# All pair products of 40 projected features: features projected in place, three store slots of 87 pairs, loads as whole 20 KB rows

## The chip, the cores and the metric

The kernel runs on one core of one Trainium2 chip. The metric is the device time in microseconds (us); of the kernel before there are three runs, with a median of 511.1 us.

## The reference

`r_x` holds 512 examples of 40 features with 128 numbers each, in fp32, and `L0_rec_W` is a 128x128 matrix. Each feature is projected by the matrix, and then each of the 780 pairs of features of an example is multiplied element by element.

```
proj = jnp.einsum('bnd,ed->bne', x, W)          # x: (512, 40, 128), W: (128, 128)
out  = proj[:, PAIR_I, :] * proj[:, PAIR_J, :]  # PAIR_I, PAIR_J = np.triu_indices(40, k=1)
```

The output has 512 x 780 x 128 numbers, 204.47 MB; the input has 10.49 MB.

## The kernel before

The 512 examples are four tiles of 128, with an example on each partition. A tile's 40 features are taken from the last to the first, in 20 groups of two. For each group TensorE transposes the two features against an identity (L172), ScalarE carries the result out of PSUM into `x_turned` (L206), TensorE multiplies it by the transposed matrix `w_turned` (L182), and ScalarE carries the projected features into `proj` (L217). VectorE then forms the pairs (L248): one instruction multiplies feature i by a run of features j, in as many pairs as fit.

The 780 pairs of a tile go out as 20 chunks of 39 pairs, also from the last to the first. A chunk is formed in one of five buffers, the slots `products0` to `products4` (19,968 bytes a partition), and SyncE issues its store when VectorE has finished it (L143 waits for `chunk_ready`, L145 issues). VectorE waits at the start of a chunk until the store that last used the slot has landed (L265, L271). So a store is 128 rows of 19,968 bytes, and there are 80 of them.

The input is loaded into `x_in`, which has two halves, one for even tiles and one for odd, in pieces of four features: 128 rows of 2,048 bytes, ten pieces a tile. SyncE issues the 20 pieces of the first two tiles at the start (L137). The pieces of the third and fourth tile are issued by ScalarE between its copies, each as soon as the groups of the piece before in that half have been turned (L211). `proj` has two halves as well. VectorE gives a half of it back when it has formed the tile's last chunk (L257), and ScalarE waits for that before it starts on the tile that will use the half (L205).

The matrix `w_in` is loaded by the first DMA of ScalarE (L199); TensorE transposes it (L162), ScalarE copies it (L201), and TensorE starts on the first group only when that copy is done (L163).

Two hardware DMA queues are in use, SyncE's (q1 in the profile) and ScalarE's (q10). A DMA of 128 rows is spread over 16 DMA engines, so that each engine has eight rows of it.

Of the kernel before, what the change touches and what calls it, by code (L numbers as in the profile page):

```python
# [5 lines left out]
P = 128  # L25
FEATURES = 40
DIM = 128
# [3 lines left out]
LOAD_FEATURES = 4  # L31
LOADS = FEATURES // LOAD_FEATURES
# [3 lines left out]
GROUPS_PER_LOAD = LOAD_FEATURES // GROUP  # L36

CHUNK = 39
CHUNKS = PAIRS // CHUNK
SLOTS = 5  # L40
ROUNDS = CHUNKS // SLOTS

assert LOADS * LOAD_FEATURES == FEATURES and GROUPS * GROUP == FEATURES
assert CHUNKS * CHUNK == PAIRS and ROUNDS * SLOTS == CHUNKS and GROUPS % 2 == 0
assert GROUP <= BANK_FEATURES and LOAD_FEATURES % GROUP == 0


def load_range(load):

    return FEATURES - (load + 1) * LOAD_FEATURES, FEATURES - load * LOAD_FEATURES  # L50


def group_range(group):

    return FEATURES - (group + 1) * GROUP, FEATURES - group * GROUP


def chunk_range(chunk):

    return PAIRS - (chunk + 1) * CHUNK, PAIRS - chunk * CHUNK  # L60


def chunk_rows(chunk):

    low, high = chunk_range(chunk)
# [8 lines left out]
def group_of(i):  # L74

    return (FEATURES - 1 - i) // GROUP


def groups_for(chunk):

    return group_of(chunk_rows(chunk)[-1][0]) + 1 if chunk >= 0 else 0


def pairwise_products(nc, x, w, out):
# [3 lines left out]
    assert x.shape[0] == tiles * P and tiles % 2 == 0 and tiles >= 4  # L88

    with ExitStack() as ctx:  # L90
# [17 lines left out]

# [6 lines left out]

        x_loaded = [[sem(f"x_loaded{half}_{k}") for k in range(LOADS)] for half in range(2)]
# [9 lines left out]
        proj_free = sem("proj_free")  # L126
# [32 lines left out]
        def _(pe):  # L159
            pe.wait_ge(identity_made, 1)  # L160
            pe.wait_ge(w_loaded, 16)
            pe.transpose(w_ps[:, :], w_in[:, :], identity[:, :]).then_inc(w_in_ps, 1)  # L162
            pe.wait_ge(w_ready, 1)  # L163

            def turn(pair, half, group):

                if group % GROUPS_PER_LOAD == 0:

                    pe.wait_ge(x_loaded[half][group // GROUPS_PER_LOAD], 16 * pair + 16)
                a, b = group_range(group)  # L170
                for n in range(a, b):
                    last = pe.transpose(turned_ps[group % 2][:, n - a, :], x_in[half][:, n, :], identity[:, :])  # L172
                last.then_inc(group_turned, 1)
# [121 lines left out]
```

## Time and profile before

| | |
|---|---|
| device time, median of 3 runs | 511.1 us (510.85 to 511.14) |
| profiled execution, first to last instruction (its span) | 508.2 us |
| difference between the two | 2.9 us |
| VectorE busy | 437.3 us (86% of the span) |
| TensorE busy | 71.3 us (14%) |
| ScalarE busy | 54.3 us (11%) |
| moved by DMA | 215.10 MB, 423 GB/s over the span |

The profile gives only the span of the profiled execution, so its time is taken as the span and the 2.9 us that the median run has beyond it. "Busy" counts the time in which an engine executes. The line of DMA digits gives the mean busy share of the 16 DMA engines in 40 slices of 12.7 us; "GB/s" is what they moved in each slice. A share can be a few hundredths above 1, since successive packets of one DMA engine overlap a little.

### The profile page before, as it was taken

To read this page: it belongs to the slowest core of one execution; us is meant where nothing else is said; L and a number is where in the kernel's file an instruction comes from. 1 tells how busy PE (TensorE), PEld (TensorE's weight loads), DVE (VectorE), ACT (ScalarE), POOL (GpSimd) and SP (SyncE) were. 2 spreads that over 40 slices of the span, in tenths; PEclk is the share of its full clock that TensorE was granted. 3 is DMA by queue.
4 is the path that set the end of the run, shared out by engine and by line. 5 is a ranking of instruction groups with operands and counts; after the bars stand their busy time and mean duration, and the time that the engine had idled before them with its cause. 6 is when DMAs were issued, how large, how long until landed. Compare 5 with 4: busy or idle time off the path is not lost.

```text
span 508.2 us, 2204 instructions
## 1 busy us (share of the span) xinstructions
PE 71.3 (14%) x481; PEld 65.4 (13%) x481; DVE 437.3 (86%) x220; ACT 54.3 (11%) x162; POOL 0.7 (0%) x6
## 2 busy tenths in 40 slices
PE   6965100000930000000660000000000000000000
PEld 5854100000920000000660000000000000000000
DVE  3999988888999999899999999999899989999900
ACT  5752000000720000000450000000000000000000
POOL 0000000000000000000000000000000000000000
PEclk9995555555875555555695555555555555555555
DMA  8999999999999999999999999999999999999996
GB/s 311 411 423 433 427 431 428 430 431 434 428 431 432 434 431 432 431 429 434 434 430 432 431 434 432 431 432 432 429 434 431 427 427 427 429 429 431 431 431 277
DMA packets 17430, 215.10 MB, mean 423 GB/s; under 512 B 1936, under 2 KB 2064, under 8 KB 7184
## 3 DMA queue, kind: packets, MB, share of 16 engines
q1 hardware_dynamic: 14400, 209.72, 96.7%
q10 hardware_dynamic: 3024, 5.31, 2.8%
q8 instruction: 2, 0.03, 0.0%
q14 instruction: 4, 0.03, 0.0%
HBM read 10.55 MB, written 204.47 MB: 423 GB/s over the span
## 4 chain that ended last, share of the span: by engine, by line
DMA 68%; DVE 21%; issue 5%; PE 1%; DVEq 0%; SPq 0%; ACT 0%; ACTq 0%
DMA out_dram<-products 67%; DVE products L248 21%; DMA w_in<-in_L_rec_W_dram 1%; PE proj_ps L182 0%; PE turned_ps L172 0%; SPq L145 0%; DVEq L248 0%; PE w_ps L162 0%; ACT proj L217 0%; ACT x_turned L206 0%; DVEq L271 0%; ACT w_turned L201 0%; SPq L144 0%; DVEq L247 0%; ACTq L205 0%
## 5 line engine op out<-in xcount | busy, mean ns | idle before, releaser
L248 DVE TENSOR_TENSOR products<-proj 128x384 f32 (+36 forms) x220 | 437.3, 2045 | 46.3 <-DMA out_dram<-products 37.3
L182 PE MATMUL proj_ps<-w_turned,x_turned 128*128 128x128 f32 x320 | 60.5, 319 | 181.5 <-ACT x_turned L206 181.3
L182 PEld LDWEIGHTS proj_ps<-w_turned,x_turned 128*128 128x128 f32 x320 | 48.9, 219 | 186.3 <-ACT x_turned L206 184.4
L206 ACT COPY x_turned<-turned_ps 128x256 f32<-128x256 f32 x80 | 30.0, 379 | 174.0 <-DVEq L257 171.9
L172 PE MATMUL turned_ps<-identity,x_in 128*128 128x128 f32 x160 | 34.4, 306 | 5.7 <-ACT proj L217 5.1
L217 ACT COPY proj<-proj_ps 128x256 f32<-128x256 f32 x80 | 29.7, 373 | 31.4 <-issue 19.0
L172 PEld LDWEIGHTS turned_ps<-identity,x_in 128*128 128x128 f32 x160 | 23.1, 161 | 6.6 <-issue 5.3
L201 ACT ACT_TABLE_LOAD x1 | 1.3, 1283 | 1.2 <-PEq L284 1.2
L162 PE MATMUL w_ps<-identity,w_in 128*128 128x128 f32 x1 | 0.4, 447 | 4.1 <-DMA w_in<-in_L_rec_W_dram 4.1
L162 PEld LDWEIGHTS w_ps<-identity,w_in 128*128 128x128 f32 x1 | 0.2, 182 | 4.0 <-issue 4.0
L201 ACT COPY w_turned<-w_ps 128x128 f32<-128x128 f32 x1 | 0.3, 265 | 2.1 <-PE w_ps L162 2.1
L155 POOL TENSOR_SCALAR_AFFINE_SELECT identity<-identity 128x128 f32<-128x128 f32 x1 | 0.3, 292 | 0.2 <-POOL identity L153 0.2
L153 POOL MEMSET identity<- 128x128 f32 x1 | 0.2, 204 | 0.3 <-POOLq L284 0.3
L284 POOL MEMSET const-bfloat16-1.0<- 128x1 bf16 x1 | 0.1, 101 | 0.0
L284 POOL MEMSET const-uint8-127<- 128x1 uint8 x1 | 0.1, 101 | 0.0
L284 POOL MEMSET const-float32-0.0<- 128x1 f32 x1 | 0.1, 98 | 0.2 <-issue 0.2
L284 POOL MEMSET const-float32-1.0<- 128x1 f32 x1 | 0.1, 98 | 0.0
## 6 DMA issues: line engine op xcount, KB each, us to landing
out_dram<-products SPq DMA_DIRECT2D x80, 2496.0 KB, 24.0
x_in<-in_r_x_dram SPq DMA_DIRECT2D x20, 256.0 KB, 6.1
x_in<-in_r_x_dram ACTq DMA_DIRECT2D x20, 256.0 KB, 29.8
w_in<-in_L_rec_W_dram ACTq DMA_DIRECT2D x1, 64.0 KB, 3.2
```

Source lines behind the costliest of these rows:

```text
L153: pool.memset(identity[:, :], 0.0).then_inc(identity_zeroed, 1)
L155: pool.affine_select(out=identity[:, :], in_=identity[:, :], compare_op=ALU.not_equal, fill=1.0, base=0, pattern=[[-1, P]], channel_multip ...
L162: pe.transpose(w_ps[:, :], w_in[:, :], identity[:, :]).then_inc(w_in_ps, 1)
L172: last = pe.transpose(turned_ps[group % 2][:, n - a, :], x_in[half][:, n, :], identity[:, :])
L182: last = pe.matmul(proj_ps[group % 2][:, k, :], x_turned[group % 2][:, k, :], w_turned[:, :], start=True, stop=True)
L201: act.copy(w_turned[:, :], w_ps[:, :]).then_inc(w_ready, 1)
L206: act.copy(x_turned[group % 2][:, :, :], turned_ps[group % 2][:, 0:GROUP, :]).then_inc(x_turned_ready, 1)
L217: act.copy(proj[:, half, a:b, :], proj_ps[group % 2][:, 0:GROUP, :]).then_inc(proj_ready, 1)
L248: last = dve.tensor_tensor(products[slot][:, place:place + count, :], proj[:, tile % 2, i:i + 1, :].broadcast_to([P, count, DIM]), proj[:, ...
L284: nc = _bacc.Bacc("TRN2", target_bir_lowering=False, num_devices=1)
```

## The change

The kernel after has one tile `feats` with two halves in place of `x_in` and `proj`: a tile is loaded into a half, and ScalarE writes each projected group over the loaded features of that group, which TensorE has already transposed. The pairs are formed from there. The freed memory goes to the slots: three of 87 pairs (44,544 bytes a partition) in place of five of 39.

Tiles 1 to 3 go out as nine chunks each, six of 87 pairs and three of 86. Tile 0 goes out as 15 chunks that grow from 30 to 69 pairs. That is 42 stores. The loads are 6: features 36 to 39, 28 to 35 and 0 to 27 of tile 0 (rows of 2,048, 4,096 and 14,336 bytes), and tiles 1, 2 and 3 whole (rows of 20,480 bytes). SyncE issues all of them. Those of tiles 2 and 3 come right behind the last store of tile 0 and of tile 1, since the half is free only when VectorE has formed all pairs of the tile in it. ScalarE issues only the matrix. `proj_free` is gone, and with it ScalarE's wait for it.

TensorE now transposes the first group before it waits for the matrix copy (`w_ready`). Its loop and those of SyncE and ScalarE over the tiles are written out; VectorE keeps a loop over tiles 1 to 3.

Of TensorE, ScalarE and VectorE the diff below shows only what is added; the lines that go are in the listing above.

```diff
-LOAD_FEATURES = 4
-LOADS = FEATURES // LOAD_FEATURES
...
-CHUNK = 39
-CHUNKS = PAIRS // CHUNK
-SLOTS = 5
-ROUNDS = CHUNKS // SLOTS
...
+FIRST_LOADS = [(36, 40), (28, 36), (0, 28)]
+SLOTS = 3
+FIRST_SIZES = [30, 34, 38, 41, 44, 47, 50, 53, 56, 59, 62, 64, 66, 67, 69]
+SIZES = [87] * 6 + [86] * 3
+SLOT_PAIRS = max(FIRST_SIZES + SIZES)
+FIRST_ROUNDS = len(FIRST_SIZES) // SLOTS
+ROUNDS = len(SIZES) // SLOTS
...
-        x_in = [sbuf(f"x_in{h}", [P, FEATURES, DIM]) for h in range(2)]
-        proj = sbuf("proj", [P, 2, FEATURES, DIM])
-        products = [sbuf(f"products{s}", [P, CHUNK, DIM]) for s in range(SLOTS)]
+        feats = sbuf("feats", [P, 2, FEATURES, DIM])
+        products = [sbuf(f"products{s}", [P, SLOT_PAIRS, DIM]) for s in range(SLOTS)]
...
-        x_loaded = [[sem(f"x_loaded{half}_{k}") for k in range(LOADS)] for half in range(2)]
+        first_loaded = [sem(f"first_loaded{k}") for k in range(len(FIRST_LOADS))]
+        tile_loaded = [sem(f"tile_loaded{half}") for half in range(2)]
...
-        proj_free = sem("proj_free")
...
-            for half in range(2):
-                for load in range(LOADS):
-                    a, b = load_range(load)
-                    sp.dma_start(x_in[half][:, a:b, :],
-                                 x[half * P:(half + 1) * P, a:b, :]).then_inc(x_loaded[half][load], 16)
-            with sp.Fori(0, tiles) as tile:
-                for chunk in range(CHUNKS):
-                    a, b = chunk_range(chunk)
-                    sp.wait_ge(chunk_ready, tile * CHUNKS + (chunk + 1))
-                    sp.nop(nofuse=True)
-                    sp.dma_start(out[bass.ds(tile * P, P), a:b, :],
-                                 products[chunk % SLOTS][:, :, :]).then_inc(stored[chunk % SLOTS], 16)
+            for k, (a, b) in enumerate(FIRST_LOADS):
+                sp.dma_start(feats[:, 0, a:b, :], x[0:P, a:b, :]).then_inc(first_loaded[k], 16)
+            sp.dma_start(feats[:, 1, :, :], x[P:2 * P, :, :]).then_inc(tile_loaded[1], 16)
+            done = 0
+            for tile in range(tiles):
+                for k, (a, b) in enumerate(first_chunks if tile == 0 else chunks):
+                    done += 1
+                    sp.wait_ge(chunk_ready, done)
+                    sp.dma_start(out[tile * P:(tile + 1) * P, a:b, :],
+                                 products[k % SLOTS][:, 0:b - a, :]).then_inc(stored[k % SLOTS], 16)
+                if tile + 2 < tiles:
+                    sp.dma_start(feats[:, tile % 2, :, :],
+                                 x[(tile + 2) * P:(tile + 3) * P, :, :]).then_inc(tile_loaded[tile % 2], 16)
             for slot in range(SLOTS):
-                sp.wait_ge(stored[slot], 16 * tiles * ROUNDS)
+                sp.wait_ge(stored[slot], 16 * (FIRST_ROUNDS + (tiles - 1) * ROUNDS))
...
+            def turn(half, group):
...
                 a, b = group_range(group)
                 for n in range(a, b):
+                    last = pe.transpose(turned_ps[group % 2][:, n - a, :], feats[:, half, n, :], identity[:, :])
                 last.then_inc(group_turned, 1)
+            def project(before, group):
...
+            def last_banks_left(before):
+                pe.wait_ge(proj_ready, before + GROUPS)
+            pe.wait_ge(identity_made, 1)
+            pe.wait_ge(w_loaded, 16)
+            pe.transpose(w_ps[:, :], w_in[:, :], identity[:, :]).then_inc(w_in_ps, 1)
+            starts = {group_of(b - 1): k for k, (a, b) in enumerate(FIRST_LOADS)}
+            pe.wait_ge(first_loaded[0], 16)
+            turn(0, 0)
+            pe.wait_ge(w_ready, 1)
+            for group in range(1, GROUPS):
+                if group in starts:
+                    pe.wait_ge(first_loaded[starts[group]], 16)
+                turn(0, group)
+                project(0, group - 1)
+            project(0, GROUPS - 1)
+            last_banks_left(0)
+            for tile in range(1, tiles):
+                pe.wait_ge(tile_loaded[tile % 2], 16 * ((tile + 1) // 2) if tile % 2 else 16 * (tile // 2))
+                turn(tile % 2, 0)
+                for group in range(1, GROUPS):
+                    turn(tile % 2, group)
+                    project(tile * GROUPS, group - 1)
+                project(tile * GROUPS, GROUPS - 1)
+                last_banks_left(tile * GROUPS)
...
...
+                act.wait_ge(group_projected, tile * GROUPS + group + 1)
+                act.copy(feats[:, tile % 2, a:b, :], proj_ps[group % 2][:, 0:GROUP, :]).then_inc(proj_ready, 1)
+            for tile in range(tiles):
+                carry_turned(tile, 0)
                 for group in range(1, GROUPS):
+                    carry_turned(tile, group)
+                    carry_projected(tile, group - 1)
+                carry_projected(tile, GROUPS - 1)
...
...
+            def multiply_chunk(tile, k, low, high, seen):
+                for i, j, count, place in chunk_rows(low, high):
+                    if group_of(i) >= seen:
+                        seen = group_of(i) + 1
+                        dve.wait_ge(proj_ready, tile * GROUPS + seen)
                     last = dve.tensor_tensor(
+                        products[k % SLOTS][:, place:place + count, :],
+                        feats[:, tile % 2, i:i + 1, :].broadcast_to([P, count, DIM]),
+                        feats[:, tile % 2, j:j + count, :], ALU.mult)
                 last.then_inc(chunk_ready, 1)
+                return seen
+            seen = 0
+            for k, (low, high) in enumerate(first_chunks):
+                if k >= SLOTS:
+                    dve.wait_ge(stored[k % SLOTS], 16 * (k // SLOTS))
+                seen = multiply_chunk(0, k, low, high, seen)
             with dve.Fori(1, tiles) as tile:
+                seen = 0
+                for k, (low, high) in enumerate(chunks):
+                    dve.wait_ge(stored[k % SLOTS],
+                                16 * ROUNDS * tile + 16 * (FIRST_ROUNDS - ROUNDS + k // SLOTS))
+                    seen = multiply_chunk(tile, k, low, high, seen)
```

SyncE's queue at the start, before. `x_in` are the loads, `products` the chunks of pairs on their way to the output, and 128x512 means 512 numbers on each partition:

```order
L131 UNCONDITIONAL_BRANCH [waits barrier_Pool_Activation_PE_DVE_SP_release]
L137 DMA x_in<-in_r_x_dram 128x512 x20
L140 UNCONDITIONAL_BRANCH
L140 ISA
L145 ISA [waits chunk_ready]
L145 DMA out_dram<-products 128x4992
L143 REGISTER_ALU
```

SyncE's queue at the start, after, up to the third store:

```order
L107 UNCONDITIONAL_BRANCH [waits barrier_Pool_Activation_PE_DVE_SP_release]
L110 DMA feats<-in_r_x_dram 128x512
L110 DMA feats<-in_r_x_dram 128x1024
L110 DMA feats<-in_r_x_dram 128x3584
L111 DMA feats<-in_r_x_dram 128x5120
L118 DMA out_dram<-products0 128x3840 [waits chunk_ready]
L118 DMA out_dram<-products1 128x4352 [waits chunk_ready]
L118 DMA out_dram<-products2 128x4864 [waits chunk_ready]
```

Twenty equal loads have become four, with the same bytes, and the first store is of 3,840 numbers a partition in place of 4,992.

SyncE's queue after, from the end of tile 0 to the load of tile 3:

```order
L118 DMA out_dram<-products 128x8576
L118 DMA out_dram<-products 128x8832
L122 DMA feats<-in_r_x_dram 128x5120
L118 DMA out_dram<-products 128x11136 x6
L118 DMA out_dram<-products 128x11008 x3
L122 DMA feats<-in_r_x_dram 128x5120
```

The loads of tiles 2 and 3 stand between stores on the same queue, where before they were on ScalarE's queue.

ScalarE's queue at the start, before (`turned_ps` and `proj_ps` are the PSUM tiles of the transposes and of the projection):

```order
L199 DMA w_in<-in_L_rec_W_dram 128x128
L201 ACT_TABLE_LOAD
L201 COPY w_turned<-w_ps 128x128 [waits w_in_ps]
L230 UNCONDITIONAL_BRANCH
L206 COPY x_turned<-turned_ps 128x256 [waits group_turned,proj_free]
L206 COPY x_turned<-turned_ps 128x256 [waits group_turned]
L211 DMA x_in<-in_r_x_dram 128x512
L217 COPY proj<-proj_ps 128x256 [waits group_projected]
```

ScalarE's queue at the start, after:

```order
L183 DMA w_in<-in_L_rec_W_dram 128x128
L185 ACT_TABLE_LOAD
L185 COPY w_turned<-w_ps 128x128 [waits w_in_ps]
L189 COPY x_turned<-turned_ps 128x256 [waits group_turned] x2
L195 COPY feats<-proj_ps 128x256 [waits group_projected]
```

The load between the copies is gone, and so is the wait for `proj_free`; the copies themselves stand as before.

## Rows read from the trace of the kernel before

**Rows 1.** The page: busy share by engine and by slice.
```profile
PE 71.3 (14%) x481; PEld 65.4 (13%) x481; DVE 437.3 (86%) x220; ACT 54.3 (11%) x162; POOL 0.7 (0%) x6
DMA  8999999999999999999999999999999999999996
GB/s 311 411 423 433 427 431 428 430 431 434 428 431 432 434 431 432 431 429 434 434 430 432 431 434 432 431 432 432 429 434 431 427 427 427 429 429 431 431 431 277
```

**Rows 2.** Waits of VectorE: who waited for whom, total us, times, longest us.
```profile
DVE products L248 <- DMA out_dram<-products: 37.3, 64, 1.4
DVE products L248 <- ACT proj L217: 8.9, 2, 7.9
```

**Rows 3.** Windows: us, busy time by engine, granted PE clock, DMA share, GB/s.
```profile
0.00:1.70 1.70, 0.00 (x0) 0.00 (x0) 0.00 (x0) 0.52 (x1) 0.70 (x6) 1.00 0.00 0
1.70:3.00 1.30, 0.00 (x0) 0.00 (x0) 0.00 (x0) 0.77 (x1) 0.00 (x0) 1.00 0.75 203
3.00:6.00 3.00, 1.41 (x5) 0.90 (x5) 0.00 (x0) 0.45 (x2) 0.00 (x0) 1.00 0.99 343
6.00:18.00 12.00, 11.90 (x90) 11.37 (x90) 9.11 (x12) 9.59 (x30) 0.00 (x0) 1.00 1.05 393
18.00:30.00 12.00, 11.20 (x91) 10.10 (x90) 12.00 (x8) 9.53 (x30) 0.00 (x0) 1.00 1.04 423
60.00:110.00 50.00, 0.00 (x0) 0.00 (x0) 43.06 (x19) 0.00 (x0) 0.00 (x0) 0.50 1.01 429
118.00:240.00 122.00, 17.46 (x120) 16.41 (x120) 111.47 (x57) 13.43 (x40) 0.00 (x0) 0.56 1.01 432
...
390.00:495.00 105.00, 0.00 (x0) 0.00 (x0) 86.19 (x35) 0.00 (x0) 0.00 (x0) 0.50 1.01 429
503.00:504.00 1.00, 0.00 (x0) 0.00 (x0) 0.00 (x0) 0.00 (x0) 0.00 (x0) 0.50 0.38 160
...
506.00:507.00 1.00, 0.00 (x0) 0.00 (x0) 0.00 (x0) 0.00 (x0) 0.00 (x0) 0.50 0.05 20
```

**Rows 4.** The page: DMA queues with packets, MB and share of 16 engines.
```profile
q1 hardware_dynamic: 14400, 209.72, 96.7%
q10 hardware_dynamic: 3024, 5.31, 2.8%
```

**Rows 5.** Loads: instructions on ScalarE's queue (ns, first to last start), and issue to landing.
```profile
L211 ACTq DMA_DIRECT2D x_in<-in_r_x_dram x20: 334/335/5746, 6.2 to 49.4; - x20
...
DMA to landing us min/median/max: 3.0/7.9/65.5
```

**Rows 6.** VectorE's largest and smallest common instruction by form: busy us, mean ns, idle.
```profile
L248 DVE TENSOR_TENSOR products<-proj 128x4992 f32 x3 | 16.1, 5358 | 1.8 <-DMA out_dram<-products 1.8
...
L248 DVE TENSOR_TENSOR products<-proj 128x384 f32 x24 | 13.3, 554 | 4.7 <-DMA out_dram<-products 4.7
```

**Rows 7.** Timeline of the opening: start us, us, engine, instruction, idle before.
```profile
0.74 0.41 ACTq L199 DMA_DIRECT2D w_in<-in_L_rec_W_dram  x1
0.75 9.87 SPq L137 DMA_DIRECT2D x_in<-in_r_x_dram  x20
...
5.04 1.11 PE L172 MATMUL turned_ps<-identity,x_in 128*128 128x128 f32 x4 [0.53 <-ACT w_turned L201]
...
9.18 54.29 DVE L248 TENSOR_TENSOR products<-proj 128x256 f32<-128x256 f32 x34 [0.99 <-ACT proj L217]
...
10.74 0.38 PE L172 MATMUL turned_ps<-identity,x_in 128*128 128x128 f32 x2
...
15.13 43.55 SPq L145 DMA_DIRECT2D out_dram<-products  x9
```

**Rows 8.** Timeline of VectorE alone, 0 to 30 us.
```profile
9.18 21.59 DVE L248 TENSOR_TENSOR products<-proj 128x256 f32<-128x256 f32 x18 [0.99 <-ACT proj L217]
```

**Rows 9.** The longest wait of ScalarE: total us, times, longest us.
```profile
ACT x_turned L206 <- DVEq L257: 171.9, 2, 101.9
```

More of the change, by code:

```diff
@@ L35, with group_of, chunk_ranges, chunk_rows @@
 GROUPS = FEATURES // GROUP
-GROUPS_PER_LOAD = LOAD_FEATURES // GROUP
-CHUNK = 39
-CHUNKS = PAIRS // CHUNK
-SLOTS = 5
-ROUNDS = CHUNKS // SLOTS
[L43 to L50, printed above, removed]
+FIRST_LOADS = [(36, 40), (28, 36), (0, 28)]
[5 more added lines that the diff above has]
+ROUNDS = len(SIZES) // SLOTS
+assert sum(FIRST_SIZES) == PAIRS and sum(SIZES) == PAIRS
+assert FIRST_ROUNDS * SLOTS == len(FIRST_SIZES) and ROUNDS * SLOTS == len(SIZES)
+assert GROUPS * GROUP == FEATURES and GROUPS % 2 == 0 and GROUP <= BANK_FEATURES
 def group_range(group):
     return FEATURES - (group + 1) * GROUP, FEATURES - group * GROUP
[L58 to L65, printed above, removed]
+def group_of(i):
+    return (FEATURES - 1 - i) // GROUP
+def chunk_ranges(sizes):
+    ranges, high = [], PAIRS
+    for size in sizes:
+        ranges.append((high - size, high))
+        high -= size
+    return ranges
+def chunk_rows(low, high):
     rows = []
@@ L71, in chunk_rows @@
     return rows
[L74 to L81, printed above, removed]
 def pairwise_products(nc, x, w, out):
@@ L159, in _ @@
         def _(pe):
[L160 to L169, printed above, removed]
+            def turn(half, group):
                 a, b = group_range(group)
                 for n in range(a, b):
-                    last = pe.transpose(turned_ps[group % 2][:, n - a, :], x_in[half][:, n, :], identity[:, :])
+                    last = pe.transpose(turned_ps[group % 2][:, n - a, :], feats[:, half, n, :], identity[:, :])
                 last.then_inc(group_turned, 1)
-            def project(pair, half, group):
-                before = pair * 2 * GROUPS + half * GROUPS
+            def project(before, group):
                 pe.wait_ge(x_turned_ready, before + (group + 1))
@@ L184, in project @@
                 last.then_inc(group_projected, 1)
-            with pe.Fori(0, tiles // 2) as pair:
-                for half in range(2):
-                    turn(pair, half, 0)
-                    for group in range(1, GROUPS):
-                        turn(pair, half, group)
-                        project(pair, half, group - 1)
-                    project(pair, half, GROUPS - 1)
-                    pe.wait_ge(proj_ready, pair * 2 * GROUPS + (half + 1) * GROUPS)
+            def last_banks_left(before):
[22 more added lines that the diff above has]
+                last_banks_left(tile * GROUPS)
         @block.scalar
@@ L201, in _, with carry_turned @@
             act.copy(w_turned[:, :], w_ps[:, :]).then_inc(w_ready, 1)
-            def carry_turned(pair, half, group):
-                act.wait_ge(group_turned, pair * 2 * GROUPS + (half * GROUPS + group + 1))
+            def carry_turned(tile, group):
+                act.wait_ge(group_turned, tile * GROUPS + group + 1)
                 act.copy(x_turned[group % 2][:, :, :], turned_ps[group % 2][:, 0:GROUP, :]).then_inc(x_turned_ready, 1)
-            def load_ahead(pair, half, load):
-                a, b = load_range(load)
-                act.dma_start(x_in[half][:, a:b, :],
-                              x[bass.ds(pair * 2 * P + (half + 2) * P, P), a:b, :]).then_inc(x_loaded[half][load], 16)
@@ L230, in _, with carry_projected @@
-            with act.Fori(0, tiles // 2 - 1) as pair:
-                for half in range(2):
-                    carry_tile(pair, half, loads=True)
-            for half in range(2):
-                carry_tile(tiles // 2 - 1, half, loads=False)
+            def carry_projected(tile, group):
+                a, b = group_range(group)
+                act.wait_ge(group_projected, tile * GROUPS + group + 1)
+                act.copy(feats[:, tile % 2, a:b, :], proj_ps[group % 2][:, 0:GROUP, :]).then_inc(proj_ready, 1)
@@ L237, in _ @@
+            for tile in range(tiles):
+                carry_turned(tile, 0)
+                for group in range(1, GROUPS):
+                    carry_turned(tile, group)
+                    carry_projected(tile, group - 1)
+                carry_projected(tile, GROUPS - 1)
         @block.vector
         def _(dve):
-            def multiply_chunk(tile, chunk):
-                slot = chunk % SLOTS
-                first_group = groups_for(chunk - 1)
-                for i, j, count, place in chunk_rows(chunk):
-                    group = group_of(i)
-                    if group >= first_group:
-                        first_group = group + 1
-                        dve.wait_ge(proj_ready, tile * GROUPS + (group + 1))
+            def multiply_chunk(tile, k, low, high, seen):
[3 more added lines that the diff above has]
+                        dve.wait_ge(proj_ready, tile * GROUPS + seen)
```

29 lines of the change are left out of this document (2 added, 27 removed).

## The prediction

> **What bounds the kernel now.** I began with the page's busy shares and slices. VectorE is busy 86%, but the DMA digits stand at 9 in all slices but the first and last, at 427 to 434 GB/s from the fourth on [rows 1]. The waits of VectorE say who leads: it waited 64 times for stores to free a slot, 37.3 us in all, and for projected features only at the very start [rows 2]. VectorE is ahead and the DMA engines are never let go, so the time is bytes over rate, plus the time before the first byte and an uneven end. The windows tell the rate of each stretch [rows 3]: nothing moves before 1.7 us; 2,048-byte load rows alone go at 393 GB/s; stores with such rows among them at 429; stores alone at 432; and in the last quarter at 429 without loads. After 503 us the share falls to 0.38, and at 506 to 507 it is 0.05, less than one of 16 engines (0.06): the engines stop on average near 504, and one works on past 507.
>
> The queue table gives the rows [rows 4]. q1's 14,400 packets are 80 stores x 128, 20 loads x 128 and 100 x 16 completions, so a row of 19,968 bytes is one packet today. The byte count barely changes, so the change can only win by fewer rows, by smoother stretches, or at the ends.
>
> **The change part by part.** Sums are made in the profiled span, 508.2 us; the median of 511.1 is 2.9 above it, which I keep.
>
> Price of a row. Per engine (a sixteenth of the rate), 19,968 bytes at 432 GB/s take 739.6 ns and 2,048 bytes at 393 take 83.4 ns. From 60 to 110 us one load goes with each store: the last of ScalarE's loads, issued at 49.4, landed 65.5 us later [rows 5], which is the time of ten such pairs. Eight rows of each at 429 GB/s take 6.569 us; less 8 x 739.6, 0.653 is left, 81.6 ns a short row. The line through 81.6 and 739.6 is 0.03672 ns a byte and 6.4 ns fixed a row; through 83.4 the fixed part is 8.4. It is zero if the store rate is a ceiling that longer rows don't lift. I take 6.4, nearest to the row that has stores in it.
>
> Stores: 10,240 rows become 42 x 128 = 5,376. That is 4,864 fewer, 304 an engine: -1.9 us (0 to -2.6). A row of 44,544 bytes should take 1,642 ns, 434 GB/s.
>
> First loads (tiles 0 and 1): 160 rows an engine at 83.4 ns are 13.3 us; after, 327,680 bytes in 32 rows, 12.0 + 0.2 = 12.2: -1.1 (0 if 393 GB/s belongs to reading and not to short rows).
>
> Later loads (tiles 2 and 3): 160 x 81.6 = 13.1 us become 16 rows, 12.0 + 0.1: -0.9 (+0.3 if reads go at 393, 13.3 us).
>
> Smoother stretches: 18 to 30 us ran at 423 where stores with loads give 429, which costs 0.2; with one data queue I count it gone (0 to -0.2). 390 to 495 ran at 429 in place of 432, 0.7 us; nothing in these rows explains it, so I take half, -0.4 (0 to -0.7).
>
> By a rule of the Trainium skill (DMA: Bandwidth & Descriptors, "Why small descriptors are slow (HBM only)") a packet has about 3 cycles of overhead on top of its 32-byte beats. As an estimate from that page's 850 MHz, 3.5 ns a row, and a 2,048-byte row would take 67 cycles, 79 ns; the trace has 81.6 and 83.4, so it bears out the kind and not the size. By the rule all row savings together come to 2.0 us and the time to about 508.5; the sum goes by the rows.
>
> The opening. The bytes still come first. By 6.0 us the windows of before have moved 0.26 + 1.03 = 1.29 MB [rows 3]; the other 4.02 of 5.31 MB (tiles 0, 1 and the matrix) take 9.3 us at 434, so loads end at 15.3. VectorE: 128x4992 takes 5,358 ns and 128x384 554 [rows 6], 1.0425 ns an element or 0.1334 us a pair. Eighteen merged instructions with 19,456 elements take 21.59 us [rows 8]; less 20.28, that is 0.07 for each. I leave the second product at 9.18 [rows 7]. It could come 0.5 earlier, since group 0's transposes need no longer wait for the matrix copy (0.53 at 5.04 [rows 7]); it could come 0.6 later, since the matrix's eight rows an engine now pass among 4,096-byte rows. The first 30 pairs then end at 9.18 + 29 x 0.1334 + 7 x 0.07 + 0.1 = 13.6. Issue adds 0.2, and 1.0 passes from issue to first byte (0.75 to about 1.7 [rows 3, 7]): 14.8, before 15.3. From there a pair costs DMA 0.151 us and VectorE 0.133 plus three or four instructions a chunk:
>
> | chunk | pairs | fit to move at | DMA free at |
> |---|---|---|---|
> | 1 | 34 | 19.7 | 19.8 |
> | 2 | 38 | 25.0 | 25.0 |
> | 3 | 41 | 30.8 | 30.8 |
> | 4 | 44 | 36.9 | 37.0 |
>
> After that the lead grows. It is tight to a tenth, so I put +0.1; one microsecond of delay at 9.18 would cost about one here, so +2 is the other end. The later loads cannot be late for TensorE: group 6, the first of the 28-feature load, was turned at 10.74 [rows 7], and that load ends at 6.0 + 1.4 MB / 434 = 9.2; even two microseconds there are hidden, since VectorE wants those features only in chunk 2.
>
> Three slots. A slot's round is three stores of 13.2 us, 39.5. In it stand the store, VectorE's 87 x 0.1334 plus up to 14 instructions, 12.6, and 1.5 of notice and issue: 27.3. The 12 us left also cover the spread of about 4 between first and last engine. Cost nothing; if this cover went, each us would show once a round.
>
> In place. Tile 2 can load only after tile 0's last pairs, near 115 us (its stores end near 133). Behind those stores it lands near 140, and turning it takes about 30. ScalarE was idle 101.9 us at a stretch for the half that VectorE held [rows 9]; VectorE needs tile 2 near 245. Slack 75 us, cost nothing. The two loads stand ahead of no store that is ready, being issued right behind one. The written-out loops of TensorE and ScalarE lie under that slack; `nop` and register work on SyncE lie in its waits for VectorE.
>
> Sum: -1.9 -1.1 -0.9 -0.2 -0.4 +0.1 = -4.4; span 503.8. The 2.9 on top gives 506.7; I round by the likelier small gain at the end to 506.6.
>
> **The rivals.**
> Reads are slow in themselves. For it: 393 GB/s is the only stretch of loads alone. Against: with stores they cost 81.6 ns a row, so most of it is the row. Then -1.9 +0 +0.3 -0.2 -0.4 = -2.2 (no idle gap, since loads end later): 508.9.
>
> The last engine comes nearer the others. It trails the mean by over 3 us, and the early stretch where two queues shared engines is one source. If half goes: 505.0.
>
> Rows of 44 KB are not moved whole. For: nothing longer than 19,968 bytes is seen. Against: those go whole. Cut in two or three, stores gain nothing: 508.5.
>
> The matrix is late. The landing of 65.5 us shows the queues taking turns row by row: 8 rows of a load needed a whole store each. Should the matrix's eight rows meet 20,480-byte rows (753 ns) and not short ones, it comes 8 x 0.67 = 5.4 us late, less 0.5 of slack: +4.9 -4.4, so 511.6. Against: its issue at 0.74 is ahead of SyncE's third [rows 7]. The Trainium skill (same page, "Queues, rings and completion order") has an engine drain a whole packet, typically 9 to 17 descriptors, from one ring before it turns to the next; by that the matrix would pass in one turn and this rival is nearly empty. The trace's alternation disagrees, so I keep it.
>
> The slower side: long store rows hold a lower rate. Place: every store; the seed of it is the 429 of the last quarter [rows 3]. Stores take 474.7 us today at their mean of 430.7 GB/s. All else gains 2.1, so it decides below 204.47 / 476.8 = 428.8 GB/s; at 426 they take 480.0, +5.3 -2.1: 514.3.
>
> **How the numbers follow.** Forecast 0.60 (own range 505.4 to 508.2), slow reads 0.12, nearer last engine 0.12, cut rows 0.05, late matrix 0.05, lower rate 0.06. The range 504.0 to 509.8 leaves out the last two and a little at the low edge. A change under 0.2%, 1.0 us, can't be told from none here. Faster by more: the first four less a little, 0.85; within: the late matrix and edges, 0.08; slower 0.07.
>
> **What would show it.** The load stretch from 6 to 14 us at about 430 GB/s rather than 393 (slow reads if not); stores at 434; q1 packets 42 x 128 + 6 x 128 + 48 x 16 = 6,912 (cut rows if more); the second product at 9.18 within 0.6 (late matrix if not); first store data at 15; no DMA share under 0.9 from 15 to 45 us; VectorE still waiting for stores; the last engine about 3 us behind. The forecast is wrong if VectorE waits for features after the opening or the store rate stays at 432 or below.

## The result and the profile after

| | before | after |
|---|---|---|
| device time, median | 511.06 us | 506.73 us (506.18 to 507.04, 4 runs) |
| ratio to before, 95% interval | | 0.9915 (0.9902 to 0.9927) |
| span of the profiled execution | 508.2 us | 504.4 us |

The change makes the kernel 4.3 us (0.85%) faster; 506.6 was forecast. The forecast of the span was 503.8.

Not all of the gain lies in the span. The runs of the kernel before that were timed beside the edits below have a median span of 508.6 to 508.7, with 2.2 us around it. The four runs of after have a median span of 504.9, with 1.8 us around it. So the span is 3.8 us shorter, and 0.4 us is saved outside it, as in every edit below. The 2.9 us that the forecast kept came from 508.2 and 511.1, a span and a median of different executions; the profiled execution of before had the shortest span of all that are listed.

The page of the kernel after, as in [rows 1], and its DMA queues, as in [rows 4]:

```profile
PE 66.4 (13%) x481; PEld 60.9 (12%) x481; DVE 431.6 (86%) x191; ACT 54.7 (11%) x162; POOL 0.7 (0%) x6
DMA  8999999999999999999999999999999999999997
GB/s 350 428 435 425 429 434 432 444 428 437 384 404 439 442 424 435 442 435 419 440 421 455 413 439 445 420 435 441 433 423 440 442 424 435 442 427 429 440 443 307
...
q1 hardware_dynamic: 6912, 214.96, 99.3%
q10 hardware_dynamic: 144, 0.07, 0.0%
```

The packet count is the 6,912 that the forecast gave for rows moved whole: 42 stores and 6 loads of 128 rows, and 48 x 16 completions. So 44,544-byte rows go as one packet. The GB/s of single slices scatter more than before, since a packet is now up to 1.6 us long and counts whole where it starts (0.7 us before). The same holds at the edges of every stretch below, so a rate over 30 us can be off by 2 to 3%. Two slices, the eleventh and twelfth (126 to 151 us), are lower than scatter explains: 384 and 404.

The stretches of after (length, busy time by engine, granted clock, DMA share, GB/s), to be laid beside [rows 3]:

```profile
1.70:3.00 1.30, 0.00 (x0) 0.00 (x0) 0.00 (x0) 0.74 (x1) 0.00 (x0) 1.00 0.77 222
3.00:6.00 3.00, 1.87 (x7) 1.33 (x8) 0.00 (x0) 0.98 (x3) 0.00 (x0) 1.00 1.07 412
6.00:14.00 8.00, 8.00 (x59) 7.73 (x58) 5.60 (x9) 5.87 (x19) 0.00 (x0) 1.00 1.01 434
14.00:30.00 16.00, 15.29 (x124) 13.82 (x122) 16.00 (x13) 13.24 (x42) 0.00 (x0) 1.00 1.02 432
60.00:110.00 50.00, 0.00 (x0) 0.00 (x0) 50.00 (x18) 0.00 (x0) 0.00 (x0) 0.50 1.01 433
118.00:150.00 32.00, 6.33 (x33) 5.92 (x34) 32.00 (x20) 3.53 (x10) 0.00 (x0) 0.52 1.02 414
150.00:240.00 90.00, 11.00 (x90) 10.16 (x88) 78.16 (x30) 9.91 (x31) 0.00 (x0) 0.59 1.00 433
270.00:360.00 90.00, 14.64 (x114) 13.75 (x112) 74.59 (x23) 12.58 (x38) 0.00 (x0) 0.59 1.00 434
390.00:495.00 105.00, 0.00 (x0) 0.00 (x0) 79.19 (x25) 0.00 (x0) 0.00 (x0) 0.50 1.00 434
474.40:504.40 30.00, 0.00 (x0) 0.00 (x0) 2.33 (x1) 0.00 (x0) 0.00 (x0) 0.50 0.89 386
```

and two stretches of the kernel before that [rows 3] has not:

```profile
118.00:150.00 32.00, 17.46 (x120) 16.41 (x120) 29.30 (x22) 13.43 (x40) 0.00 (x0) 0.71 1.00 431
...
478.20:508.20 30.00, 0.00 (x0) 0.00 (x0) 5.36 (x1) 0.00 (x0) 0.00 (x0) 0.50 0.86 367
```

The loads of the opening go at 434 GB/s in place of 393. Stores alone go at 433 to 434 in place of 432, and the 429 of the last quarter is gone. From 118 to 150 us the rate is 414, where before it was 431: by these rates 32 x (431 - 414) / 431 = 1.3 us are lost there. In it lie the last store of tile 0 and the load of tile 2 behind it. And the end is shorter: in the last 30 us before it moved 367 x 30 = 11.0 MB and after 11.6, which at 434 GB/s is 1.3 us less idling.

The edges can be taken out: the trace has a start, a duration and a size for each packet, so its bytes can be spread evenly over its duration. The time lost in a stretch is then its length less its bytes at 434 GB/s. In us ("the rest to 470" is 150 to 235 and 290 to 470 us):

| lost against 434 GB/s | 0 to 14 | 14 to 115 | 115 to 150 | 235 to 290 | the rest to 470 | from 470 | sum |
|---|---|---|---|---|---|---|---|
| before | 3.8 | 1.9 | 0.25 | 0.3 | 1.9 | 4.4 | 12.6 |
| after | 2.8 | 0.9 | 2.05 | 0.2 | 0.3 | 2.6 | 8.8 |

The difference of the sums, 3.8 us, is that of the two spans. So the stretch with the load of tile 2 costs 1.8 us more than before, and the end 1.9 less. The loss with the load is sharply placed. The store rows of 35,328 bytes that start between 132 and 133 us take 1.94 us in the mean where 1.31 is usual. The load's rows of 20,480 bytes take 0.78 us between 136 and 138, but 1.1 to 1.2 between 138 and 140; those of the next load that start from 259 to 265 us take 0.76 to 0.78.

VectorE in the opening and its waits, as in [rows 7, 8] and [rows 2]:

```profile
7.13 0.29 DVE L212 TENSOR_TENSOR products<-feats 128x128 f32<-128x128 f32 x1 [7.13 <-ACT feats L195]
8.41 0.89 DVE L212 TENSOR_TENSOR products<-feats 128x256 f32<-128x256 f32 x2 [0.99 <-ACT feats L195]
9.59 51.89 DVE L212 TENSOR_TENSOR products<-feats 128x512 f32<-128x512 f32 x32 [0.29 <-ACT feats L195]
```

```profile
DVE products L212 <- DMA out_dram<-products: 36.6, 22, 7.5
DVE products L212 <- ACT feats L195: 8.4, 3, 7.1
```

The second product starts at 8.41, 0.77 earlier than before, so the matrix was not late. VectorE still waits for stores, 36.6 us in all, only in 22 longer waits in place of 64.

### The profile page after: what moved, and what is told of

Read it like the earlier page. It is cut to its first block, busy times and chain, and to the rows that moved or that the text cites. A ratio compares the mean times of both kernels' runs of the same rounds, so it can differ in the third digit from the quotient of the medians.

```text
span 504.4 us, 1671 instructions
## 1 busy us (share of the span) xinstructions
PE 66.4 (13%) x481; PEld 60.9 (12%) x481; DVE 431.6 (86%) x191; ACT 54.7 (11%) x162; POOL 0.7 (0%) x6
## 3 DMA queue, kind: packets, MB, share of 16 engines
q1 hardware_dynamic: 6912, 214.96, 99.3%
## 4 chain that ended last, share of the span: by engine, by line
DMA 46%; DVE 41%; issue 5%; DVEq 2%; PE 1%; ACT 0%
DMA out_dram<-products 45%; DVE products L212 41%; DVEq L69 1%; DMA w_in<-in_L_rec_W_dram 1%; PE proj_ps L149 1%; DVEq L212 0%; PE turned_ps L140 0%; DVEq L211 0%; DVEq L224 0%; PE w_ps L158 0%; ACT feats L195 0%; DVEq L227 0%
## 5 line engine op out<-in xcount | busy, mean ns | idle before, releaser
L212 DVE TENSOR_TENSOR products<-feats 128x384 f32 (+49 forms) x191 | 431.6, 2331 | 45.1 <-DMA out_dram<-products 36.6
L140 PE MATMUL turned_ps<-identity,feats 128*128 128x128 f32 x160 | 33.3, 297 | 213.8 <-DMA feats<-in_r_x_dram 213.3
L149 PE MATMUL proj_ps<-w_turned,x_turned 128*128 128x128 f32 x320 | 56.9, 304 | 0.3 <-ACT x_turned L189 0.2
L140 PEld LDWEIGHTS turned_ps<-identity,feats 128*128 128x128 f32 x160 | 22.1, 156 | 214.6 <-issue 213.6
L149 PEld LDWEIGHTS proj_ps<-w_turned,x_turned 128*128 128x128 f32 x320 | 45.5, 205 | 4.8 <-ACT x_turned L189 2.0
L195 ACT COPY feats<-proj_ps 128x256 f32<-128x256 f32 x80 | 29.8, 372 | 11.8 <-PE proj_ps L149 6.6
```

Of the source, the lines that this page charges most:

```text
L140: last = pe.transpose(turned_ps[group % 2][:, n - a, :], feats[:, half, n, :], identity[:, :])
L149: last = pe.matmul(proj_ps[group % 2][:, k, :], x_turned[group % 2][:, k, :], w_turned[:, :], start=True, stop=True)
L195: act.copy(feats[:, tile % 2, a:b, :], proj_ps[group % 2][:, 0:GROUP, :]).then_inc(proj_ready, 1)
L212: last = dve.tensor_tensor(products[k % SLOTS][:, place:place + count, :], feats[:, tile % 2, i:i + 1, :].broadcast_to([P, count, DIM]), f ...
```

## The experiments

All are edits of the changed kernel, and ratios are to the kernel before, timed beside them. The yardstick first.

### The changed kernel again

No edit.

> The changed kernel once more, unchanged, as the yardstick for the runs beside it, and to see what repeats. Theory A (rows): the gain of 4.3 us is fewer rows and a smoother opening, the loss between 118 and 142 us of the first profile (414 GB/s from 118 to 134) was chance; then this profile shows 433 there and the loads of tile 2 take 6.2 us. Theory B (the load behind the last store of tile 0 disturbs the stores): 118 to 142 shows about 414 again. Time by both 506.2 to 507.1.

Measured: 506.45 us, ratio 0.9909 (0.9894 to 0.9924). The stretch is there again:

```profile
6.00:14.00 8.00, 8.00 (x54) 7.81 (x52) 5.47 (x9) 5.50 (x17) 0.00 (x0) 1.00 1.02 439
14.00:30.00 16.00, 15.22 (x124) 13.81 (x122) 16.00 (x13) 13.13 (x42) 0.00 (x0) 1.00 1.01 428
118.00:150.00 32.00, 5.69 (x25) 5.32 (x26) 32.00 (x21) 2.95 (x8) 0.00 (x0) 0.50 1.03 415
300.00:380.00 80.00, 0.00 (x0) 0.00 (x0) 73.22 (x32) 0.00 (x0) 0.00 (x0) 0.50 1.00 434
```

From 115 to 150 us 2.2 us are lost, with the bytes spread as above. So the slow stretch belongs to the kernel and is no chance of one execution.

### Stores of 39 pairs

```diff
-SLOTS = 3
-FIRST_SIZES = [30, 34, 38, 41, 44, 47, 50, 53, 56, 59, 62, 64, 66, 67, 69]
-SIZES = [87] * 6 + [86] * 3
+SLOTS = 5
+FIRST_SIZES = [39] * 20
+SIZES = [39] * 20
```

> The changed kernel with five slots of 39 pairs in every tile, as before the change; loads stay whole rows on SyncE's queue. It has 10,240 store rows, 4,864 more. Theory A, rows at 6.4 ns: stores cost 1.9 us more, so 508.6, and the store stretches go at 432 GB/s. Theory C, the row length of the stores is worth nothing and the gain came from the loads and the queue: 506.7. Theory D, all of the gain is the stores: 511.

Measured: 509.82 us, ratio 0.9978 (0.9969 to 0.9987), so 3.4 us above the yardstick, more than theory A's 1.9. The same four stretches:

```profile
6.00:14.00 8.00, 8.00 (x60) 7.74 (x59) 5.81 (x9) 6.13 (x19) 0.00 (x0) 1.00 1.01 435
14.00:30.00 16.00, 15.29 (x123) 13.95 (x122) 16.00 (x11) 13.25 (x41) 0.00 (x0) 1.00 0.98 415
118.00:150.00 32.00, 4.67 (x21) 4.31 (x22) 25.81 (x19) 2.24 (x6) 0.00 (x0) 0.50 1.01 406
300.00:380.00 80.00, 0.00 (x0) 0.00 (x0) 73.66 (x38) 0.00 (x0) 0.00 (x0) 0.50 1.01 432
```

The rate of stores alone is as theory A has it, 432 against 434: over the 475 us of stores, 2.2 us. The rest has three places. From 14 to 30 us it is 415 against 428, 16 x 13 / 428 = 0.5 us (0.3 with the bytes spread): the loads now end at 15, and 39 pairs are not formed by then, while 30 are. That is what the small first chunks are worth. The 406 against 415 from 118 to 150 us is an effect of the edges: with the bytes spread the two kernels lose the same there, 2.2 us. What is slower is the stretch of the next load, that of tile 3: from 235 to 290 us this kernel loses 1.25 us and the yardstick 0.25, of which 0.2 is the store rows. The end gives another 0.4. With rows at 2.0 to 2.2 that makes 3.5, near the 3.4.

### Loads in 2,048-byte rows

```diff
-FIRST_LOADS = [(36, 40), (28, 36), (0, 28)]
+FIRST_LOADS = [(a, a + 4) for a in range(36, -1, -4)]
...
+            for a in range(36, -1, -4):
+                sp.dma_start(feats[:, 1, a:a + 4, :], x[P:2 * P, a:a + 4, :]).then_inc(tile_loaded[1], 16)
```

and the same for tiles 2 and 3, behind the stores.

> The changed kernel with every tile loaded in ten pieces of 2,048-byte rows, all on SyncE's queue; stores stay at 87 pairs. Theory A: 272 more rows an engine at 6.4 to 8.4 ns, so 1.7 to 2.3 us more, 508.4 to 509.0, with 393 GB/s from 6 to 14 us. Rival, 393 GB/s came from two queues interleaving and not from short rows: the stretch from 6 to 14 us goes at 409 or more and the time is under 508.2.

Measured: 508.25 us, ratio 0.9951 (0.9937 to 0.9965), 1.8 us above the yardstick; theory A had 1.7 to 2.3. The rows, with the last 30 us of this kernel:

```profile
6.00:14.00 8.00, 8.00 (x60) 7.73 (x58) 5.73 (x10) 5.99 (x19) 0.00 (x0) 1.00 1.05 393
...
118.00:150.00 32.00, 5.50 (x29) 5.04 (x30) 32.00 (x22) 3.12 (x9) 0.00 (x0) 0.52 1.02 427
```

```profile
476.40:506.40 30.00, 0.00 (x0) 0.00 (x0) 2.34 (x1) 0.00 (x0) 0.00 (x0) 0.50 0.84 363
```

and the last 30 us of the yardstick:

```profile
474.80:504.80 30.00, 0.00 (x0) 0.00 (x0) 2.35 (x1) 0.00 (x0) 0.00 (x0) 0.50 0.89 383
```

With one queue alone the short rows again go at 393 GB/s, the figure of [rows 3], so it comes from the row and neither from reading (whole rows are read at 434 to 439) nor from two queues. But the sum is right by a different road than the forecast's: the opening costs 8 x 46 / 439 = 0.8 us from 6 to 14 us alone, and the end costs 30 x (383 - 363) / 434 = 1.4 us, while the stretch from 118 us is 1 us better than in the yardstick, at 427. With the bytes spread, 0 to 14 us costs 1.0 us more, the end 1.4 more, the stretch of tile 3's load 0.4 more, and 115 to 150 us 1.2 less.

### Both together

The two edits above in one kernel.

> Five slots of 39 pairs and loads in 2,048-byte rows together: the rows of the kernel before, but features in place and one data queue (SyncE's). Theory A: what is left of the difference to the kernel before is the queue and the tail. Both row terms back give 506.7 + 1.9 + 2.0 = 510.6. If mixing two queues cost the kernel before something of its own (rows of up to 1.1 us in its opening, the last engine 3 us behind), this is 1 us or more under it, 509 to 510; if not, it is within 0.5 of it.

Measured: 511.31 us, ratio 1.0003 (0.9994 to 1.0012): the time of the kernel before, 510.79 in the median beside it. 3.4 + 1.8 = 5.2, and together 4.9. So the size of stores and loads accounts for all of the gain. What is left of the change (features in place, one data queue, later loads in a lump, the order of the first transposes, no `proj_free`, written-out loops) is worth nothing in sum, but the sum has parts that cancel. Time lost against 434 GB/s, in us, as above:

| | 0 to 14 | 14 to 115 | 115 to 150 | 235 to 290 | the rest to 470 | from 470 | sum |
|---|---|---|---|---|---|---|---|
| before | 3.8 | 1.9 | 0.25 | 0.3 | 1.9 | 4.4 | 12.6 |
| this kernel | 3.7 | 0.9 | 2.05 | 1.25 | 1.45 | 4.4 | 13.8 |
| stores of 39 pairs | 2.8 | 1.6 | 2.25 | 1.25 | 1.4 | 3.3 | 12.6 |
| loads in 2,048-byte rows | 3.8 | 0.7 | 0.95 | 0.7 | 0.3 | 4.3 | 10.7 |
| yardstick | 2.8 | 0.8 | 2.15 | 0.25 | 0.3 | 2.8 | 9.2 |

Against the kernel before, the lumped later loads cost this kernel 2.7 us in their two stretches. It gets back 1.0 from 14 to 115 us, where the kernel before has these loads, 0.5 in the rest, and 0.4 outside the span. The 0.5 is the 429 of the last quarter: with the same row sizes it is 431 to 432 here and in the kernel above, so its cause is not the row. Its stretch and its end:

```profile
118.00:150.00 32.00, 4.56 (x20) 4.19 (x21) 25.86 (x19) 2.23 (x6) 0.00 (x0) 0.50 1.01 406
```
```profile
479.50:509.50 30.00, 0.00 (x0) 0.00 (x0) 5.36 (x1) 0.00 (x0) 0.00 (x0) 0.50 0.86 367
```

The stretch is slow although its loads are in 2,048-byte rows, so the 427 above was not owed to short rows alone. The end is as ragged as before: the last engine's last row lands 3.2 us behind the mean of the sixteen, as in the kernel before, on one data queue now. So the two queues were not what kept it behind.

### Later loads on ScalarE's queue

```diff
+                if tile >= 2:
+                    act.wait_ge(chunk_ready, len(first_chunks) + (tile - 2) * len(chunks))
+                    act.dma_start(feats[:, tile % 2, :, :],
+                                  x[tile * P:(tile + 1) * P, :, :]).then_inc(tile_loaded[tile % 2], 16)
```

with SyncE's loads of these tiles removed.

> The changed kernel with the whole-row loads of tiles 2 and 3 issued by ScalarE in place of SyncE, at the same moment (when VectorE has formed the tile's last pairs). Bytes and rows are the same. If two data queues cost something of their own: rows alternate, the stretch of the load goes under 430 GB/s, the engines drift further apart and the time is 0.5 to 1.5 us above the changed kernel. If only the row count matters: the same within 0.3 us. The load lands earlier by alternation, which nothing needs.

Measured: 506.70 us, ratio 0.9919 (0.9906 to 0.9933), 0.25 above the yardstick: the same within what can be told. The stretches of the two loads:

```profile
117.00:127.00 10.00, 0.00 (x0) 0.00 (x0) 10.00 (x11) 0.00 (x0) 0.00 (x0) 0.50 1.00 382
127.00:147.00 20.00, 8.05 (x51) 7.50 (x52) 18.74 (x11) 5.31 (x16) 0.00 (x0) 0.60 1.00 431
...
235.00:265.00 30.00, 5.35 (x24) 4.98 (x25) 22.50 (x19) 2.62 (x8) 0.00 (x0) 0.50 0.99 415
```

and the first two in the yardstick:

```profile
117.00:127.00 10.00, 0.00 (x0) 0.00 (x0) 10.00 (x10) 0.00 (x0) 0.00 (x0) 0.50 0.94 404
127.00:147.00 20.00, 2.69 (x11) 2.32 (x12) 20.00 (x12) 1.08 (x3) 0.00 (x0) 0.50 1.03 404
```

With the bytes spread, this kernel loses 1.2 us from 115 to 130 and 0.1 from 130 to 150, and the yardstick 0.1 and 2.0. The slow stretch moved to an earlier start with the load. So it follows the load, on either queue. Here tile 3's load has one too: 1.0 us from 235 to 290, against 0.25.

### Tile 0 in chunks of 87

```diff
-FIRST_SIZES = [30, 34, 38, 41, 44, 47, 50, 53, 56, 59, 62, 64, 66, 67, 69]
+FIRST_SIZES = [87] * 6 + [86] * 3
```

> The changed kernel with tile 0 in nine chunks of 87 and 86 pairs like the others, so the first store waits for 87 pairs. VectorE has them at 8.4 + 87 x 0.133 + 13 x 0.07 = 20.9, data moves 1.2 later, 22.1, and the loads end at 15.0: 7.1 us idle, less 6 x 8 rows x 6.4 ns = 0.3 saved and 0.3 of small gaps: 513.2. If the DMA engines could make up the gap later (they were not the bound), the time stays near 507.

Measured: 512.69 us, ratio 1.0035 (1.0023 to 1.0047), 6.2 above the yardstick. Its stretches:

```profile
14.00:15.00 1.00, 1.00 (x10) 0.96 (x10) 1.00 (x2) 0.93 (x4) 0.00 (x0) 1.00 0.72 307
15.00:22.00 7.00, 6.71 (x54) 6.07 (x53) 7.00 (x7) 5.96 (x19) 0.00 (x0) 1.00 0.02 5
22.00:30.00 8.00, 7.57 (x62) 6.97 (x63) 8.00 (x4) 6.33 (x21) 0.00 (x0) 1.00 1.04 446
```

Seven microseconds of idle DMA, and the end 6.2 later in the median (7.1 in the profiled execution): a gap there is not made up. This is the price of large slots without small first chunks, and larger than the whole gain.

### Without the later loads

```diff
+                if tile == 1:
+                    pe.wait_ge(tile_loaded[1], 16)
+                else:
+                    pe.wait_ge(chunk_ready, len(first_chunks) + (tile - 2) * len(chunks))
```

with SyncE's loads of tiles 2 and 3 left out, so that these tiles are computed from what lies in the halves.

> The loads of tiles 2 and 3 are left out (5.24 MB of 215; TensorE turns what lies in the half instead, at the same moment); all stores and all other work stay. If every byte moved is on the path: 2 x 6.1 = 12.2 us less, and another 1.1 if the slow load of the first profile is gone with it: 494.5, or 493.4. If VectorE were the bound after the opening it would stay near 506.

Measured: 492.83 us, 13.6 under the yardstick. By bytes 5.24 MB are 12.1 us; the other 1.5 is about the size of the slow stretch, which is gone (with the bytes spread, 0.3 us are lost from 115 to 150, in place of 2.2):

```profile
118.00:150.00 32.00, 15.02 (x114) 13.95 (x113) 32.00 (x20) 12.59 (x38) 0.00 (x0) 0.77 1.02 437
```

### Matrix before the first transposes

```diff
-            turn(0, 0)
             pe.wait_ge(w_ready, 1)
+            turn(0, 0)
```

> The changed kernel with the group 0 transposes again behind the wait for the matrix copy. VectorE's second product comes 0.5 to 0.7 us later (9.0 in place of 8.4). First 30 pairs fit to move at 14.7, loads end at 15.0: the first store is not late, but from chunk 2 on VectorE and DMA run level, so about 0 to 0.4 us more, 506.7 to 507.1. If the opening had no slack at all: +0.7.

Measured: 506.32 us, ratio 0.9909 (0.9893 to 0.9924): no difference to the yardstick, though VectorE's second product started 0.55 us later than in the yardstick:

```profile
8.99 0.89 DVE L212 TENSOR_TENSOR products<-feats 128x256 f32<-128x256 f32 x2 [0.99 <-ACT feats L195]
...
14.00:30.00 16.00, 15.23 (x124) 13.83 (x122) 16.00 (x13) 13.22 (x41) 0.00 (x0) 1.00 0.98 413
```

That is no slack in the opening: from 14 to 30 us the rate is 413 against 428, and with the bytes spread this kernel loses 0.5 us more than the yardstick from 14 to 60 us. It is shorter by 0.3 at the end, which differs by that much between kernels with equal loads. So the median, with single runs up to 0.7 us apart, does not show the delay, and the trace does.

### Later loads in five pieces, in two, and tiles swapped

```diff
+                    for b in range(FEATURES, 0, -FEATURES // PIECES):
+                        a = b - FEATURES // PIECES
+                        sp.dma_start(feats[:, tile % 2, a:b, :],
+                                     x[(tile + 2) * P:(tile + 3) * P, a:b, :]).then_inc(tile_loaded[tile % 2], 16)
```

with `PIECES` 5 or 2. The third kernel has whole rows and takes the last two tiles in the order 3, 2.

> The changed kernel with the loads of tiles 2 and 3 in five pieces each (4,096-byte rows); tiles 0 and 1 stay. Theory F (a load in long rows right behind stores slows stores and load around 132 to 141 us, in both traces of the changed kernel and not in the run with 2,048-byte pieces): 118 to 142 us comes back to about 425 GB/s, 1.2 to 1.6 us are gained less 64 rows x 5.5 ns = 0.35: 505.2 to 505.6. Rival, the slow stretch has to do with the time or the address and only happened not to show: 0.35 us more, 506.8.

> The changed kernel with the loads of tiles 2 and 3 in two pieces each (10,240-byte rows). Theory F with a loss that grows with the row: about half of the loss at 118 to 142 us is left, 505.9 to 506.2. Rival: as with five pieces, no effect beyond 0.1 us for the added rows, 506.6.

> The changed kernel that takes the fourth tile of examples third and the third fourth (input and output addresses alike); instructions and sizes are the same. If the slow stretch hangs on the moment (the load behind the last store of tile 0), it stays at 118 to 142 us with about 414 and 392 GB/s; if it hangs on the address read, it moves to the load at 260 us. Time 506.5 either way.

Measured: 506.66 us (ratio 0.9916, 0.9902 to 0.9929), 506.07 (0.9907, 0.9892 to 0.9924) and 506.18 (0.9909, 0.9894 to 0.9924). The stretch in the three, in this order:

```profile
118.00:150.00 32.00, 5.57 (x25) 5.20 (x26) 32.00 (x22) 2.85 (x8) 0.00 (x0) 0.50 1.00 404
```
```profile
118.00:150.00 32.00, 6.63 (x41) 6.10 (x42) 32.00 (x20) 4.18 (x13) 0.00 (x0) 0.55 1.02 413
```
```profile
118.00:150.00 32.00, 6.12 (x27) 5.75 (x28) 32.00 (x21) 2.98 (x8) 0.00 (x0) 0.50 1.02 412
```

Theory F falls: the slow stretch is there with rows of 4,096, 10,240 and 20,480 bytes; with the bytes spread, all three lose 2.0 to 2.1 us from 115 to 150. It isn't the address read either. Two pieces has the lowest median of all, 0.4 us under the yardstick, which the overlapping intervals don't let one call a gain.

### Later loads spread over four stores

```diff
+                    if 1 <= tile < tiles - 1 and k < PIECES:
+                        high = FEATURES - k * (FEATURES // PIECES)
+                        low = high - FEATURES // PIECES
+                        sp.dma_start(feats[:, (tile + 1) % 2, low:high, :],
+                                     x[(tile + 1) * P:(tile + 2) * P, low:high, :]).then_inc(tile_loaded[(tile + 1) % 2], 16)
```

with `PIECES = 4`.

> The changed kernel with the loads of tiles 2 and 3 in four pieces each (5,120-byte rows), one behind each of the first four stores of the next tile, so that load and stores mix over 50 us as in the kernel before. Theory G (a load in one lump between stores causes the slow stretch, spread out it doesn't, since the kernel before shows 429 where it mixes them): 118 to 150 us at 430 or more, 1.3 us less and 0.3 more for 48 rows an engine: 505.3 to 505.6. Rival (whatever is read at the first turn from storing to loading is slow, lump or not): the slow stretch stays or moves with the first piece, 506.3 to 506.8.

Measured: 513.51 us, ratio 1.0035 (1.0017 to 1.0054): 7 us above the yardstick, which neither theory had. Its 12 executions lie between 508.8 and 514.4; those of the other kernels are within 1.4 us of each other. No engine of computation was late (VectorE waited for features only in the opening). The stretches with pieces, and the end:

```profile
118.00:150.00 32.00, 0.00 (x0) 0.00 (x0) 32.00 (x20) 0.00 (x0) 0.00 (x0) 0.50 1.01 418
150.00:200.00 50.00, 0.52 (x3) 0.55 (x4) 41.69 (x15) 0.00 (x0) 0.00 (x0) 0.50 1.00 426
245.00:280.00 35.00, 0.00 (x0) 0.00 (x0) 32.31 (x18) 0.00 (x0) 0.00 (x0) 0.50 0.99 420
481.70:511.70 30.00, 0.00 (x0) 0.00 (x0) 2.40 (x1) 0.00 (x0) 0.00 (x0) 0.50 0.70 302
505.00:508.00 3.00, 0.00 (x0) 0.00 (x0) 0.00 (x0) 0.00 (x0) 0.00 (x0) 0.50 0.20 88
```

The rate is down for as long as pieces pass, and then the end is ragged: a share of 0.20 from 505 to 508 us is three engines of 16 that still work while the others are done, and the last 30 us moved 9.1 MB against 11.5 in the yardstick, 5.6 us at 434 GB/s. The other 1.7 us or so are lost between 115 and 390. When the engines came apart can be read from the sixteen landings of each store. From the first to the last of them it is 1.6 us before the pieces, grows with each piece of tile 2 to 5.7 at 199 us, stays there to 265, grows with the pieces of tile 3 to 10.3 at 341, and stays there. In the yardstick it goes from 1.3 to 3.0. So the engines come apart while loads and stores alternate on the queue, and stay apart. Spreading the loads is the wrong direction.

## Why the prediction was right, step by step

**What bounds the kernel** was read rightly: DMA is never let go. Leaving 5.24 MB out took 13.6 us off, and a gap of 7 us in the opening came back as 6.2 at the end. (Below, what a stretch lost or gained is taken with the bytes spread over the packets.)

**Stores, forecast -1.9** by 6.4 ns a row, with -0.6 for smoother stretches. The row part holds: from 290 to 390 us, stores alone, the kernel before loses 0.54 us and after 0.11, which is 2.0 over the 475 us of stores. Undoing the store size alone costs 3.4, and the rest is no price of a row: the worth of the small first chunk (0.3 to 0.5), since the faster loads end before 39 pairs are ready, but not before 30 are; a slow stretch with tile 3's load (0.8); and the end (0.4). The 429 of the last quarter, of which I took half as gone, is 434 in the changed kernel, and 431 to 432 with stores of 39 pairs, so about 0.5 of it came from something else than rows, and no run tells what.

**First loads, forecast -1.1,** came out at -1.0 by 14 us and a little more behind it: 434 from 6 to 14 us, against 393. At equal bytes 4.0 MB after 6 us now take 9.3 in place of 10.2, 0.9, and by 6.0 us 0.23 MB more had been moved, another 0.5. Slow reads, the first rival, is out: whole rows are read at the rate of stores.

**Later loads, forecast -0.9,** is the step that failed. The price of a row was right for the first loads, but a whole tile's load in one lump between stores brings a slow stretch: from 115 to 150 us after loses 1.8 us more than before. Nothing in the rows of before shows it, since there the loads lay as short rows of a second queue among the stores. The term came out at about -0.9 + 1.8 = +0.9.

**The end, forecast 0, and half of its 3.3 us in the second rival,** paid for that: from 470 us on, after loses 1.9 us less than before. The last engine, forecast about 3 us behind, ends 1.7 behind the mean of the sixteen (2.0 in the yardstick), and 3.2 before. So what the second rival describes did happen, at a chance of 0.12, and the slow stretch hid it. Loads in short rows bring the ragged end back (363 GB/s in the last 30 us against 383), and so it goes with the loads. The sum of 4.4 was near the measured 4.3 because these two missing terms cancel, which is luck.

**The opening, forecast +0.1:** the second product came at 8.41, 0.77 early, and the matrix not late. "Tight to a tenth" holds: with the product 0.55 us later, 0.5 us more are lost by 60 us, though the median does not show it. As it stands, 0.2 us are lost from 14 to 30 us.

**Costed at nothing** were three slots, features in place, the loops and the order of the first transposes. VectorE waits for stores and never for features after the opening, and with short rows on both sides the whole rest of the change measures 1.0003, as a sum of parts that cancel: the lumped loads cost 2.7 us, and lower losses elsewhere and less time outside the span give back most of it. Cut rows are out by the packet count; a lower rate of long rows by 434.

**The span's surroundings** were taken as 2.9 us and left alone; they are 2.2 before and 1.8 after. The forecast span of 503.8 was 0.6 below the profiled one and 1.1 below the median of the four runs; the time was met to 0.1 because this error ran the other way. That is luck too.

The rule on packets of about 3 cycles (the Trainium skill, DMA: Bandwidth & Descriptors, "Why small descriptors are slow (HBM only)") would have given, by the forecast's estimate, 508.5, outside the measured spread; 2,048-byte rows at 393 to 394 GB/s are 83 ns in three kernels, on one data queue and on two, against the 79 estimated from it.

**What stays open** is the slow stretch itself. The runs show that it comes with the load (gone without it, moved with it), on either queue, whatever the address read, and for rows of 2,048 to 20,480 bytes: 2.0 to 2.2 us with whole rows on SyncE's queue, 1.3 on ScalarE's, and 0.9 in one of the two kernels with 2,048-byte rows. Why tile 3's load costs next to nothing with stores of 87 pairs on one queue, and about 1 us with stores of 39 pairs or on the second queue, no run tells; nor why alternating loads and stores drive the engines apart. Why short load rows make the last engine later is open as well; that they do rests on three profiles (before, and the two kernels with short load rows), which lose 4.3 to 4.4 us from 470 us on, while those of the edits with whole-row loads of tiles 0 and 1 lose 2.4 to 3.3, but for the one that spreads its later loads.

## What to carry to other kernels

When DMA is never let go, price each DMA row: on its engine 0.037 ns a byte plus 6 to 8 ns fixed, as the line through two row sizes gave here, and count rows; larger slots pay only if the first chunks stay small enough to be ready when the loads end. Look at two more places that bytes over rate does not show: how far the last DMA engine ends behind the mean, and the stretch where a load lies among stores. Take the time around the span from the same execution as the span. When packets are long, spread their bytes over their duration before two stretches are compared.

## What the runs showed that I had not expected

A load between stores on one queue costs more than its bytes: 13.6 us for 5.24 MB (12.1 at 434 GB/s), and cut into eight pieces that alternate with stores it costs 7 us more and leaves three engines working 5 us after the others. The two queues of the kernel before, which pass row by row, mixed the same loads with stores at 429 GB/s and show no such stretch. The second queue alone is not the remedy, since whole rows on it lose 1.3 and 1.0 us.
